# Top-k attention in 56 tiles of 128 rows of heads and tokens in place of 64 tiles of 112, with the masks as bfloat16 products over all 128 rows

## The reference, cut to what matters

```
Q = (x_text @ Wq).reshape(Bb, Tt, H, DH)            # 16 batches, 112 tokens, 4 heads of 32
K = (x_vision @ Wk).reshape(Bb, Gg, H, DH)          # 375 context rows of 192 features
scores = jnp.einsum('bthd,bghd->bhtg', Q, K) / np.sqrt(DH)
scores = jnp.where(vision_mask[:, None, None, :], scores, -jnp.inf)
topv, topi = jax.lax.top_k(scores, K_TOP)           # K_TOP = 32
probs = jax.nn.softmax(topv, axis=-1)
attn = jnp.zeros_like(scores).at[bi, hi, ti, topi].set(probs)
attn_mean = attn.mean(axis=1)                       # mean over the heads
V = x_vision @ Wv
c_t = jnp.einsum('btg,bgd->btd', attn_mean, V) * text_mask[..., None]
```

## Time and profile before

| what | value |
|---|---|
| runs, us | 2418.9, 2416.46, 2422.77 |
| median, us | 2418.9 |
| profiled execution, us | 2417.03 |
| its span, us | 2415.2 |
| mean granted clock of PE | 0.897 |
| busy, share of the span | PE 87%, POOL 34%, DVE 63%, ACT 29% |
| chain that ended last | PE 66%, DVE 21%, POOL 5%, ACT 3% |

### The profile page before, as it was taken

How to read it: one execution, slowest core, us unless ns; L and a number is a source line. 1 busy time by engine, 2 the same in 40 slices (tenths; PEclk the granted TensorE clock), 3 DMA queues, 4 the chain that set the end, 5 groups by cost and what they waited for, 6 DMA issues and landing times.

```text
span 2415.2 us, 37733 instructions
## 1 busy us (share of the span) xinstructions
PE 2096.2 (87%) x15300; PEld 1468.4 (61%) x15300; DVE 1532.5 (63%) x3079; ACT 701.6 (29%) x1351; POOL 811.6 (34%) x729
## 2 busy tenths in 40 slices
PE   6988989999999978999999999987667677879986
PEld 2333347777666657888788878776535455446632
DVE  7998945556343325555555555566389989737556
ACT  6445324343212222222222222222122222121232
POOL 3243339966400025444444444433081000013201
PEclk7768789999899989999999999999866757989998
DMA  5212172222010037001000100100061101220001
GB/s 153 77 67 96 61 164 83 59 72 60 5 53 1 1 116 171 11 1 68 1 1 26 44 1 1 51 1 1 1 159 29 35 25 33 67 68 1 0 1 31
DMA packets 67182, 114.48 MB, mean 47 GB/s; under 512 B 34153, under 2 KB 58722, under 8 KB 65794
## 3 DMA queue, kind: packets, MB, share of 16 engines
q1 hardware_dynamic: 67010, 112.07, 16.2%
HBM read 91.56 MB, written 33.34 MB: 52 GB/s over the span
## 4 chain that ended last, share of the span: by engine, by line
PE 66%; DVE 21%; POOL 5%; ACT 3%; issue 3%; DMA 2%; SPq 1%; POOLq 0%; DVEq 0%; ACTq 0%
PE PS L1529 8%; PE PS L1545 8%; PE PS L1278 5%; PE PS L1256 4%; DVE top L2286 4%; PE PS L1446 4%; DVE w_s L2295 4%; PE PS L2173 2%; PE PS L2163 2%; PE PS L2102 2%; PE PS L1474 2%; PE PS L1504 2%; PE PS L1556 2%; DVE st_h L689 2%; PE PS L877 2%
## 5 line engine op out<-in xcount | busy, mean ns | idle before, releaser
L287 POOL TENSOR_SCALAR ln_ve<-ln_mv 128x2 f32<-128x2 f32 (+1 forms) x91 | 21.8, 240 | 1157.0 <-DVE ln_mv L271 1156.9
L1728 DVE TENSOR_TENSOR p_x<-PS,cols 128x1024 f32<-128x1024 f32 x112 | 129.3, 1216 | 147.9 <-PE PS L1491 147.8
L1792 POOL TENSOR_TENSOR q_x<-q_f,cols 128x2048 f32<-128x2048 f32 x56 | 208.7, 3745 | 11.2 <-ACT q_f L1646 11.2
L1087 DVE TENSOR_REDUCE XD<-PS 112x2 f32<-112x750 f32 x128 | 119.8, 939 | 95.7 <-PE PS L877 95.2
L455 PE MATMUL PS<-bc_parts,ident 96*128 96x448 bf16 x256 | 105.4, 516 | 43.1 <-DVE st_h L689 28.9
L1046 ACT ACTIVATE e_t<-PS 125x672 f32<-125x672 f32 x128 | 93.6, 731 | 158.0 <-PE PS L890 158.0
L1335 DVE SCALAR_TENSOR_TENSOR XA<-PS,gate_w,XA 112x256 f32<-112x256 f32 x128 | 56.0, 479 | 125.6 <-PE PS L1278 125.6
L877 PE MATMUL PS<-enc_w,q_s 32*112 32x375 f32 x512 | 131.1, 538 | 2.2 <-DVE XD L1087 2.2
L1616 ACT ACTIVATE wb<-PS,cols 128x256 f32<-128x256 f32 x224 | 91.0, 473 | 139.7 <-PE PS L1529 139.7
L2062 PE MATMUL PS<-dg,e_p 112*125 112x112 f32 x384 | 78.3, 394 | 60.4 <-ACT dg L2241 60.4
L890 PE MATMUL PS<-q_s,enc_w 32*125 32x112 f32 x1536 | 123.3, 291 | 2.6 <-ACT e_t L1046 2.6
(11 more groups left out here) (357 smaller groups left out, 4715.2 us busy)
## 6 DMA issues: line engine op xcount, KB each, us to landing
k_full_scratch<-k_scratch SPq DMA_DIRECT2D x112, 112.0 KB, 2.9
v_all_scratch<-v_st SPq DMA_DIRECT2D x16, 750.0 KB
v_t<-v_all_scratch SPq DMA_DIRECT2D x16, 750.0 KB
t_ring<-k_full_scratch SPq DMA_DIRECT2D x8, 784.0 KB, 15.4
enc_w<-in_enc_w SPq DMA_DIRECT2D x2, 3072.0 KB, 11.3
wc<-in_enc_w SPq DMA_DIRECT2D x2, 3072.0 KB, 11.4
k_all_scratch<-k_st SPq DMA_DIRECT2D x16, 375.0 KB
enc_w<-k_all_scratch SPq DMA_DIRECT2D x64, 93.8 KB, 3.5
```

The lines of the kernel that those rows point to most:

```text
L1087: dve.tensor_reduce(nm_w[0:T, g % 4, 64 * half + 16:64 * half + 49:32], PS[0:T, 2 * half:2 * half + 2, 0:S2], AX.X, ALU.max, negate=True). ...
L1728: last = dve.tensor_tensor(p_x[:, m, :, :, :], ps[1][:, m * P:(m + 1) * P].rearrange("p (h i) -> p h i", i=16).unsqueeze(2) .to_broadcast( ...
L1792: last = pool.tensor_tensor(q_x[:, c, :, :].rearrange("p t (h i) -> p t h i", i=16), q_f[:, k % 2, c, :].rearrange("p (t i) -> p t i", i=1 ...
```

## The change

Heads and tokens of two neighbouring batches are taken as one list of 2 x 448 rows, which is cut into seven tiles of 128, so that 56 tiles replace 64. Tile 7u + 3 holds 64 rows of batch 2u and 64 of batch 2u + 1 (`tile_parts`); the others lie in one batch. What follows from this:

- `q_z` holds the queries of two batches, with each head's 32 rows in the columns of that head and zeros elsewhere, so that a score product runs over all 128 rows. ACT fills it with four copies per two batches (`spread_queries`), POOL clears it once.
- The mask is a product over all 128 rows in bfloat16 (`mskb` and `ident16`, which gets a fourth block), in place of float32 over 32 rows.
- DVE works on 28 pairs of tiles. One negation serves both tiles of a pair, and reciprocal and scaling (now with a second tensor, `tmk` in tile order with 1/4 in it) come behind every pair.
- dg is a piece of a loaded pattern `shift` (one more DMA) scaled by 1/sum. attend(b) takes the four tiles in which b has rows; it has 12 products as before.
- The order on PE, per pair i: scores of tiles 2i + 2 and 2i + 3; then attend and gather of the batch whose last tile was in pair i - 1, and values; then the keys that `keys_at` gives. keys(0) and keys(1) come before all scores. ACT: two exponentials, the copies of attend, gather and values, the copy of keys, the spread of queries, dg.
- POOL's norms are grouped by quarters, with the same instructions.

The core of the diff:

```diff
@@ s4x_pool
             pool.wait_ge(xa_copied, B // 2)
+            link(pool.memset(q_z[:, :, :, :], 0.0))
             pool.memset(msk8[:, :], 1).then_inc(e_prep, 1)
@@ s4x_load
+            sp.dma_start(shift[:, :], dr["shift"]).then_inc(em_loaded, 16)
@@ before s4x_pe
+        TILES = B * XH * T // P
+        STEPS_T = TILES // 2
+        def first_tile(b):
+            return 7 * (b // 2) + 3 * (b % 2)
+        def tile_parts(n):
+            u, r = divmod(n, 7)
+            if r == 3:
+                return [(2 * u, slice(0, 64)), (2 * u + 1, slice(64, P))]
+            return [(2 * u + (r > 3), slice(0, P))]
+        def finished(i):
+            return [b for b in range(B) if (first_tile(b) + 3) // 2 == i]
+        def keys_at(i):
+            return [b for b in range(2, B) if first_tile(b) // 2 - 2 == i]
@@ s4x_pe
-                    pe.matmul(ps[h][0:T, 0:S2], q_e[r, b * T:(b + 1) * T], k_e[r, b % 2, :],
-                              start=True, stop=False)
-                    pe.matmul(ps[h][0:T, 0:S2], ident[r, 32 * h + b:32 * h + b + 1].to_broadcast([32, T]), mskb[r, :],
-                              start=False, stop=True).then_inc(x_s_ready, 1)
+            def scores(n):
+                parts = tile_parts(n)
+                pe.wait_ge(m_used, m_count("k", parts[-1][0]) + 1)
+                pe.wait_ge(qz_ready, n // 7 + 1)
+                if n >= 4:
+                    pe.wait_ge(x_exp, n - 3)
+                at = P * (n % 7)
+                for b, s in parts:
+                    queries = q_z[:, n // 7 % 2, :, :].rearrange("p z m -> p (z m)")[:, at + s.start:at + s.stop]
+                    pe.matmul(ps[n % 4][s, 0:S2], queries, k_e[:, b % 2, :], start=True, stop=False)
+                    row_mask = ident16[:, b:b + 1].to_broadcast([P, s.stop - s.start])
+                    last = pe.matmul(ps[n % 4][s, 0:S2], row_mask, mskb[:, :], start=False, stop=True)
+                last.then_inc(x_s_ready, 1)
+            for i in range(STEPS_T):
+                if i + 1 < STEPS_T:
+                    scores(2 * i + 2)
+                    scores(2 * i + 3)
+                for b in finished(i - 1):
                     attend(b)
                     gather(b)
                     if b % QB == QB - 1:
                         values(b // QB)
+                for b in keys_at(i):
+                    keys(b)
@@ s4x_act
+            def spread_queries(u):
+                if u >= 2:
+                    act.wait_ge(x_s_ready, 7 * (u - 1))
+                for h in range(XH):
+                    r = slice(32 * h, 32 * h + 32)
+                    last = act.copy(q_z[r, u % 2, :, h * T:(h + 1) * T],
+                                    q_e[r, 2 * u * T:2 * (u + 1) * T].rearrange("p (z t) -> p z t", t=T))
+                last.then_inc(qz_ready, 1)
+            for i in range(STEPS_T):
+                for n in (2 * i, 2 * i + 1):
                     act.wait_ge(x_first, n + 1)
+                    act.activation(e_p[:, n % 8, :], ps[n % 4][:, 0:S2], ACT.Exp,
+                                   bias=neg_m[:, n % 4:n % 4 + 1]).then_inc(x_exp, 1)
+                for b in finished(i - 1):
+                    copy_attention(b)
+                    copy_context(b)
+                for b in keys_at(i):
+                    copy_keys(b)
+                    if b % 2 == 0 and b >= 4:
+                        spread_queries(b // 2)
+                act.wait_ge(x_rs, i + 1)
+                for n in (2 * i, 2 * i + 1):
+                    off = 96 - 16 * (n % 7)
+                    last = act.activation(dg[:, n % 8, :], shift[:, off:off + T], ACT.Copy,
+                                          scale=e_rs[:, n % 8:n % 8 + 1])
                 last.then_inc(x_dg, 1)
@@ s4x_dve
-                            for a, h, n in pair:
-                                link.after(found[a])
-                                found[a] = link.mark(dve.tensor_scalar(neg_m[:, h:h + 1], top8[:, a, 0, 0:1], -1.0,
-                                                                       None, ALU.mult))
+                        link.after(found[1])
+                        m = 2 * i % 4
+                        found = [link.mark(dve.tensor_scalar(neg_m[:, m:m + 2], top8[:, :, 0, 0], -1.0, None,
+                                                             ALU.mult))] * 2
```

More of the change, by code:

```diff
@@ L2087, in s4x_pe @@
             keys(0)
+            keys(1)
             scores(0)
-            for b in range(B):
-                if b + 1 < B:
-                    keys(b + 1)
-                    scores(b + 1)
+            scores(1)
+            for i in range(STEPS_T):
[3 more added lines that the diff above has]
+                for b in finished(i - 1):
                     attend(b)
@@ L2104, in film @@
                 last.then_inc(ready, 1)
-            pe.wait_ge(x_exp, B * XH)
+            pe.wait_ge(x_exp, TILES)
             pe.wait_ge(e_prep, 5)
```

187 lines of the change are left out of this document (89 added, 98 removed).

## The result

The changed kernel takes **2459.9 us** (median of 4 runs, 2455.6 to 2467.4) where the kernel before takes 2417.7 beside it: ratio 1.017, 95% interval 1.0143 to 1.0197. I had said 2424, with a range up to 2447. The profiled execution took 2455.6, its span is 2453.6, against 2415.2 before: 38.4 us more. It is the fastest of the four, so what is read from it explains 38.4 us and not the 42 between the medians.

The account below looks back on a forecast made before the run. DVE was taken to bound the top-k stage: 2043.9 without waits plus 32.9 of waits gives 2076.8 against 2072.0, +4.8; with the end +6.8, onto 2417.0: 2424 us, 8-in-10 range 2400 to 2447.

Parts of the forecast that it names:

- The first cluster of waits: DVE's waits up to pair 9, after keys(2) lands late: 1.0, 0.6, 0.8, 8.6, 1.0 and 3.7, together 15.7 us.
- The regular clusters: DVE's waits at pairs 13 to 15 and 20 to 22, behind late ctx_f transfers: 8.6 us each.
- The wait for the first exponentials: In a regular cluster, DVE's multiply waits for scores and exponentials behind the late keys: 3.9 us.
- The next: In a regular cluster, pair 8's multiply waits behind attend(3), gather, values and copies at full clock: 3.7 us.
- clock stays up: Rival: denser PE work keeps full clock, regular clusters lose 4.6 us; 2407 us in all, chance 0.27.
- Attend's price: PE's attend per batch, taken from the kernel before: 5.35 us at half clock, 2.84 at full.
- The end: After DVE's last pair, attend(15) comes later and PE bounds what follows: 1.2 to 2.9 us, taken as 2.0.
- The start: DVE's pair 3 begins at about 1808.4, set by ctx_f(2) landing at 1802.1 and the path behind it.
- PE becomes the bound: Rival: half clock throughout gives 2467 us, a half-clock share 2443; chances 0.21 for 2443, 0.05 for worse, to 2467.
- point of decision: PE becomes the bound where about half its work runs at half clock; the stage before had some 58%.
- The chain is covered: Rival: ctx_f lands early enough and ACT isn't held, so waits go to nothing: 2391 us, chance 0.10.
- My own sign for being wrong: Sum of DVE's waits after 1810 under 17 or over 50 us; also limits on pair cost and stage clock.

Follow-up runs that it names:

- The first experiment: Changed kernel with ctx_f(b + 1) issued on SP ahead of the wait for gather(b - 2): 2397.1 us, ratio 0.9897 to the kernel before.
- all the edits: Changed kernel with ctx_f early, ctx_f(2) ahead of weights, filling ahead of attend(14), POOL's norms in pieces, attend's 64-row products last: 2388.8 us.

## Why the prediction was wrong

**What held.** A pair costs 9.44 us (9.42). From gather to keys it is 6.0 to 6.2 at the three places that were named (5.9). The first cluster of waits up to pair 9 is 17.4 (15.7). The clusters stand where they were put, at pairs 7, 14 and 21 and the one behind each, by the mechanism that was named: a transfer behind gather, ACT standing at the keys' copy, DVE's multiply behind. The first experiment shows that mechanism by taking it away. I had listed three waits of keys behind a gather; there are seven more of 3.5 to 5.4 us after keys(2), behind none of which DVE loses more than 2.1.

**What was mis-sized.** The profiled execution is 31.8 us over the sum of 2423.8: 23.4 in the waits (56.3 for 32.9), 4.8 at the end, 1.2 at the start, 0.5 in the pairs, the rest behind the stage.
- *The regular clusters*, 8.6 us each in the sum, measured 17.3 and 18.6. This term failed, and with it the forecast. The wait for the first exponentials is 5.5 and 6.8 in place of 3.9. The next is 11.8 in place of 3.7, near my own price for half clock, 10.9, with attend's 1.37 us more on it, 12.3. (The terms written out for the 3.7, 11.2 less 7.97, give 3.2; the 0.5 between them is explained nowhere and changes little.) I had priced attend, gather and values behind the scores at full clock; the row from 1940 to 1960 has 0.50 with PE busy for 17 of 20 us. That was to be had from before: the earlier trace rows shows the same, and I used it against the rival "clock stays up" but not against my own sum.
- *Attend's price.* I took the price of 12 products over 112 rows; with changes between 128 and 64 rows it is 3.67 and 6.72. No attend of before had such a change within it, so no bound from one could be made; but the prediction didn't even list it as an unknown. It cost more than its 0.8 to 1.4 us per attend: with one change in place of five the time falls by 24 or 38 us.
- *The end*, +2.0 in the sum, is +6.8 to the convolution. I saw that attend(14) starts later, and priced it at 5 and gather at 2; behind 6 us of PE's idle time they were 6.7 and 2.9. The film products I had at half clock, 5.4 for 5.58. So attend(15) comes 7.0 behind DVE's end and not 2.7 to 4.4.
- *The start*, 1808.4 against 1809.6, was partly luck. The path from the landing was sized right: keys(2) at 1801.76 (1802.1), DVE's multiply at 1806.53 (1807.0 by the sum). But a second bound stands at nearly the same time, and the prediction didn't have it: POOL's operations had set DVE back so far that the landing held it for 0.3 us only, and then held its multiply for 1.7 us more. So the landing alone, taken away, gives nothing: with ctx_f(2) early pair 3 still starts 35.0 us behind the first max. The earlier trace rows show no sign of this but a multiply of over 2 us.

**The rivals.** "PE becomes the bound", half clock throughout, gave 20.3 for a regular cluster and 2443 to 2467: the measured 2460 lies there, and I had given this 0.26. Its point of decision was the share of PE's work at half clock. Two of its figures are off: the full-clock sum is 8.4 + 2 x 6.17 + 1.9 = 22.6 and not 24, and the windows of before give some 49% of PE's work (66% of its busy time) at half clock, not 58%. And the share of the stage as a whole is no guide: it hardly moved (granted clock 0.67 before, 0.69 after), while DVE's waits grew by 47 us. What counts is the clock inside a cluster (0.50 from 1940 to 1960). "The chain is covered", 2391, is what comes out when ctx_f is sent early (2397) or with all the edits (2389): the gain of the 28 pairs is real. My own sign for being wrong, waits above 50 us, came true: 53.7 listed.

## What to carry to other kernels

When a change takes work off the engine that sets the pace, follow each in-order queue to the first place where the new order leaves a transfer no slack, and price what PE does behind that idle time at half clock, the products further behind included. Keep PE's products of one height together; with the short ones last the kernel was faster where the transfer was late, and no difference was shown where it was early. For each bound, look for what stands just behind it: here the landing of a transfer and POOL's hold fell together, and taking the landing away gave the start nothing. Look for two-operand operations of DVE that grow from 0.5 to over 2 us: POOL holds them up, and no list of waits names it.

## What the hardware showed

- A change between 64-row and 128-row products costs attend 0.27 us at half clock, and 0.13 to 0.28 at full (6.72, 6.18, 5.64 and 3.67, 3.31, 3.05 for 5, 3, 1 changes).
- Behind the late transfers, with 64-row products in front or between, the clock stays at 0.50 in whole attends; with them last it mostly rises earlier, and the time is 14 us lower for the same work. Why isn't shown.
- 24 us more of busy PE time in the stage made the kernel 29 us faster, through the clock (0.69 to 0.86).
- DVE's multiply of two SBUF tensors stands until POOL's tensor operation has ended, and DVE's loop falls into step with POOL's: 11.6 us for each of two pairs in a row, in place of 9.44, while POOL repeats every 11.56.
